# A decoder layer with routed experts: its opening in another order, with rows copied within SBUF, smaller pieces and ready-made constants

## What is computed

```python
x = x + attention(layernorm(x))        # 16 heads of 16, bias -|i - j| * 0.5 ** head, softmax over 1024 keys
x = x + cross_attention(layernorm(x))  # one head of 256, 77 context rows
x = x + experts(layernorm(x))          # 8 experts 256 -> 1024 -> 256, the two best per row
```

## Time and profile before

| | |
|---|---|
| median of 3 runs | 1537.01 us (1536.56 to 1537.97) |
| the profiled execution | 1541.59 us, its span 1539.7 us |
| mean granted TensorE clock | 0.981 of full speed |
| PE busy | 1481.3 us, 96% of the span |
| DVE, ACT, POOL busy | 1172.5, 1014.2, 415.0 us |
| first maximum's matmul / first score's matmul | 35.06 / 91.90 us from the span's start |

### The profile page before, as it was taken

One profiled execution on the slowest core, in us unless ns is written; L12 is line 12 of the kernel. 1 busy time (PEld: TensorE's weight loads), 2 busy tenths in 40 slices (PEclk: granted clock), 3 DMA queues, 4 the chain that ended last, 5 costly groups with the idle time before them and its releaser, 6 DMA issues.

```text
span 1539.7 us, 28797 instructions
## 1 busy us (share of the span) xinstructions
PE 1481.3 (96%) x9670; PEld 890.0 (58%) x9670; DVE 1172.5 (76%) x2578; ACT 1014.2 (66%) x1826; POOL 415.0 (27%) x457
## 2 busy tenths in 40 slices
PE   5899999999999999999999999999999999999997
PEld 3433443244444334444443444335999999999996
DVE  5889887788887778888877877854778887665563
ACT  3056666677655757665567575778677788776673
POOL 3200130002110014211003210023537655544453
PEclk9799999999999989999989999999999999999998
DMA  5750350330432504205042230133568888899993
GB/s 143 129 120 13 45 121 34 41 43 4 66 71 55 97 22 77 35 9 124 29 69 55 44 43 10 48 121 127 165 190 230 259 234 240 240 269 260 255 269 79
DMA packets 90404, 172.55 MB, mean 112 GB/s; under 512 B 14467, under 2 KB 48515, under 8 KB 90256
## 3 DMA queue, kind: packets, MB, share of 16 engines
q1 hardware_dynamic: 73120, 142.98, 37.0%
q0 software_dynamic: 15744, 26.54, 8.4%
q10 hardware_dynamic: 1392, 1.18, 0.4%
HBM read 134.27 MB, written 36.00 MB: 111 GB/s over the span
## 4 chain that ended last, share of the span: by engine, by line
PE 84%; DVE 8%; issue 3%; ACT 3%; DMA 1%; SPq 1%; POOL 0%; ACTq 0%; POOLq 0%; DVEq 0%
PE ps L1257 15%; PE ps L1231 15%; PE ps L1217 12%; PE ps L1459 4%; PE ps L1478 4%; PE ps L1479 3%; PE ps L1457 3%; PE ps L1458 3%; PE ps L1480 3%; DVE sums L1683 2%; PE ps L1363 2%; PE ps L1329 2%; PE ps L1220 2%; PE ps L1461 2%; PE ps L1276 1%
## 5 line engine op out<-in xcount | busy, mean ns | idle before, releaser
L1503 ACT ACTIVATE prob<-ps 128x512 f32<-128x512 f32 x1024 | 562.4, 606 | 305.2 <-PE ps L1217 175.0
L1257 PE MATMUL ps<-stacked_k,stacked_q 112*128 112x512 bf16 x1024 | 396.4, 393 | 17.1 <-DVE rmax L1683 4.0
L1683 DVE CUSTOM_DVE_ANT_0 sums<-ps,ramps 128x512 bf16<-128x512 f32 x480 | 328.9, 685 | 81.3 <-PE ps L1257 73.8
L1685 DVE TENSOR_REDUCE rmax<-ps 128x1 f32<-128x512 f32 x480 | 327.3, 687 | 73.7 <-PE ps L1257 69.3
L1217 PE MATMUL ps<-stacked_q,stacked_k 115*128 115x512 bf16 x1024 | 363.4, 384 | 4.2 <-ACT prob L1503 1.8
L1257 PEld LDWEIGHTS ps<-stacked_k,stacked_q 112*128 112x128 bf16 x1024 | 100.2, 99 | 334.8 <-DVE rmax L1683 117.7
L1231 PE MATMUL ps<-prob,values 128*32 128x512 f32 x2048 | 275.5, 610 | 1.3 <-issue 0.8
L2128 POOL DMA_INDIRECT out<-yo,token_of x71 | 139.6, 1966 | 189.8 <-DVE yo L2010 138.8
L1634 ACT ACTIVATE hid<-ps,w_now 128x256 f32<-128x256 f32 (+1 forms) x312 | 124.7, 452 | 88.3 <-PE ps L1459 59.6
L1217 PEld LDWEIGHTS ps<-stacked_q,stacked_k 115*128 115x128 bf16 x1024 | 99.8, 98 | 100.4 <-ACT prob L1503 53.9
L1478 PE MATMUL ps<-w_high,hid_high 128*128 128x256 f32 x512 | 149.1, 291 | 1.5 <-DVE sums L2004 1.5
(11 more groups left out here) (246 smaller groups left out, 2399.4 us busy)
## 6 DMA issues: line engine op xcount, KB each, us to landing
w_now<-in_w SPq DMA_DIRECT2D x78, 514.0 KB
w_now<-in_w SPq DMA_DIRECT2D x78, 512.0 KB
stacked_q<-parts_of_rows SPq DMA_DIRECT2D x90, 128.0 KB, 6.3
stacked_k<-parts_of_rows SPq DMA_DIRECT2D x90, 128.0 KB, 6.8
xi<-expert_rows SPq DMA_DIRECT2D x71, 130.0 KB, 3.0
parts_of_rows<-q_part SPq DMA_DIRECT2D x21, 256.0 KB, 5.6
parts_of_rows<-k_part SPq DMA_DIRECT2D x21, 256.0 KB, 5.7
b_now<-in_b SPq DMA_DIRECT2D x39, 128.0 KB
```

The costliest lines, as they stand in the source:

```text
L1257: m = e.matmul(ps[:, bank, :], qa[i][0:MAX_ROW, hh, qt * P:(qt + 1) * P], ka[i][0:MAX_ROW, hh, kc * BANK:(kc + 1) * BANK], start=True, sto ...
L1503: e.activation(prob[:, u % NPROB, :], ps[:, score_bank(u), :], ACT.Exp, scale=SLOPE ** (k[0] % NG * HG + k[3])).then_inc(sem["exp"], 1)
L1683: e.tensor_tensor_reduce(sums_16[:, :], of, ramp_beside(1 - qt % 2, qt % 4), 1.0, -3.0e38, ALU.add, ALU.max, into).then_inc(sem["maxed"], 1)
L1685: e.tensor_reduce(into, of, AX.X, ALU.max).then_inc(sem["maxed"], 1)
```

## The change

- **Layer norm in fours.** The statistics, reciprocal root and shift of sequence 0 are taken for tiles 0 to 3 and then for tiles 4 to 7; of the first four tiles ACT normalises two and DVE two (`normed`), and PE waits for each tile by itself.
- **Transfers of the opening.** The weights come in three pieces (q and k of heads 0 to 7, q and k of heads 8 to 15, values), the first between the rows' second and third transfer. The identity, the scales and the bias come from ACT's queue. The position rows are passed ready made in bf16 and go from the input to the stacks.
- **Rows without DRAM.** `direct` copies the parts of group 0 from SBUF to the stacks, 12 transfers for each half; five of them (q high and mid, first half) are started by POOL, the others by SP. Group 1's stacks are also filled from SBUF, in 12 transfers, and without a wait for the context's. To make that possible the channels of q and k are in the order (d, h) within a group; the later `spread` transfers therefore read 8 KB in one piece where it was four times 2 KB.
- **PE kept running.** 14 matmuls of 512 columns on zeros at the start and 5 after the first statistics. They write to a bank that nobody reads yet.
- **Order.** POOL no longer makes low parts of the weights; DVE does. The two projections of the other half (heads 0 to 7) stand behind the first rows. The eight context transfers go from POOL's queue to SP's, behind the 16 of the stacks 1 and 2 and group 1. The context products start after 32 maxima where it was 48.

```diff
+DIRECT = 2.8
+WARM, WARM_AFTER = 14, 5
...
-FIRST_ALONE = 3 * UNITS // 4
+FIRST_ALONE = UNITS // 2
+FIRST_BY_ACT = 2
...
+def by_pool(a, n, ch):
+    return a == 0 and n < 2 and ch == 0
...
     def prepare_first():
-        yield from layer_norm("pre", 0, WHOLE, FORE)
-        add("scale_q")
+        for tt in range(*FORE):
+            add("stats", "pre", 0, tt)
+        add("aggr", "pre", 0, FORE)
+        add("rstd", "pre", 0, FORE)
+        add("scale_q", 0)
         add("scale_bias")
         add("w_high", 0)
         add("w_low", 0)
+        add("shift", "pre", 0, FORE)
+        for tt in range(*FORE):
+            add("norm" if tt < FIRST_BY_ACT else "normed", "pre", 0, tt)
         for c in range(DC):
-            yield from x_parts(0, c, 0)
+            add("x_turn", 0, c, 0)
+            add("x_high", 0, c, 0)
+        for tt in range(*AFT):
+            add("stats", "pre", 0, tt)
+        for c in range(DC):
+            add("x_low", 0, c, 0)
+        add("aggr", "pre", 0, AFT)
+        add("rstd", "pre", 0, AFT)
+        add("specials")
+        for a in range(2):
+            for i in range(p.parts(("proj",))):
+                p.add_part(i, "proj", 0, 0, a, 0)
+            for n, kind in enumerate(("high", "rest", "mid", "low")):
+                add(kind, 0, 0, a, 0)
+                if kind != "rest":
+                    add("direct", a, n - (n > 0), 0)
+            if a == 0:
+                add("shift", "pre", 0, AFT)
         for tt in range(*AFT):
             add("norm", "pre", 0, tt)
-
-        yield from project(0, 0, 0, 0)
+        add("fill")
+        yield 0
         for c in range(DC):
-            yield from x_parts(0, c, 1)
-        yield from project(0, 0, 1, 0)
+            add("x_turn", 0, c, 1)
+            add("x_high", 0, c, 1)
+            empty("x_low", 0, c, 1)
+            yield 0
+        flush()
+        add("scale_q", 1)
         for i in range(1, DC + 1):
             add("w_high", i)
-            add("w_low_late", i)
+            add("w_low", i)
         for a in range(2):
             yield from project(0, 0, a, 1)
-        for ch in range(NCH):
-            add("first_half", ch)
+            flush()
+            for n in range(NPART):
+                add("direct", a, n, 1)
         split.add((0, 0))
-        now["spread"] = 1
         spread_when_ready()
+        add("context_in")
...
+        spec_rows = t["c_spec"].bitcast(BF16)
...
-        by_row = lambda rows: rows.rearrange("(h d) n -> d h n", d=DH)
+        by_row = lambda rows: rows.rearrange("(d h) n -> d h n", d=DH)
...
+        def direct_rows(e, a, n, ch):
+
+            cols, part = slice(ch * BANK, (ch + 1) * BANK), ("high", "mid", "low")[n]
+            if (a, n) == (1, 0) and ch == 0:
+                e.wait_ge(sem["k_ones"], 1)
+            rows = "early_rows" if by_pool(a, n, ch) else ("first_rows", "spread0")[ch]
+            e.wait_ge(sem[part], p.upto(part, 0, 0, a, ch))
+            for j, pair in enumerate(PAIRS):
+                if pair[a] == n:
+                    e.dma_start((qa, ka)[a][0][DH * j:DH * (j + 1), :, cols], split[n][a][first_group, 0, cols]).then_inc(sem[rows], 16)
...
+            rows_of_x(0)
+            rows_of_x(1)
+            piece_in(0)
+            rows_of_x(2)
+            rows_of_x(3)
+            e.dma_start(ramp_in, t["c_ramps"].rearrange("a p n -> p a n")).then_inc(sem["ramps_in"], 16)
+            position_rows(0)
+            for i in range(1, DC + 1):
+                piece_in(i)
+            e.dma_start(bv_all[:, :], t["bv"].broadcast_to([P, D])).then_inc(sem["values_bias_in"], 16)
...
+                elif kind == "context_in":
+
+                    e.wait_ge(sem["w_low"], DC + 1)
+                    for i, (w, b) in enumerate((("xwk", "xbk"), ("xwv", "xbv"), ("xwq", "xbq"))):
+                        e.dma_start(cw[i], t[w].rearrange("(c p) n -> p c n", p=P)).then_inc(sem["context_in"], 16)
+                        e.dma_start(cbias[i], t[b]).then_inc(sem["context_in"], 16)
+                    e.dma_start(cx[0:CTX, :, :], t["ctx"].rearrange("b c d -> c b d")).then_inc(sem["context_in"], 16)
+                    e.dma_start(xwo[:, :, :], t["xwo"].rearrange("(c p) n -> p c n", p=P)).then_inc(sem["context_in"], 16)
...
-                        e.wait_ge(sem["positions"], 32)
-                        e.wait_ge(sem["spread0"], spread_in(0))
-                        e.wait_ge(sem["context_in"], 8 * 16)
                         for other in range(1, NSET):
                             position_rows(other)
+                        for part in ("high", "mid", "low"):
+                            e.wait_ge(sem[part], p.upto(part, 0, 0, 1, NCH - 1))
+                        for j, pair in enumerate(PAIRS):
+                            for a, rows in enumerate((qa, ka)):
+                                e.dma_start(rows[1][DH * j:DH * (j + 1), :, :], split[pair[a]][a][next_group, 0, :]).then_inc(sem["spread1"], 16)
+                        continue
...
+            def warm(n):
+
+                for _ in range(n):
+                    e.matmul(ps[:, AV_BANK, :], sums_16[:, 0:P], sums_16[:, :], start=True, stop=True)
+
+            e.wait_ge(sem["first_set"], 1)
+            warm(WARM)
+            e.wait_ge(sem["aggr"], 1)
+            warm(WARM_AFTER)
...
-                    if (mo, a) == (0, 0) and first:
-                        e.wait_ge(sem["x_low"], p.upto("x_low", b, DC - 1, ch))
+                    if (mo, a) == (0, 0):
+                        e.wait_ge(sem["x_low"], p.upto("x_low", b, part, ch))
                     if b == 0 and first:
-                        if mo == 0:
-                            e.wait_ge(sem["w_low"], 1)
-                        else:
-                            e.wait_ge(sem["w_low_late"], 1)
+                        e.wait_ge(sem["w_low"], mo + 1)
...
+            e.dma_start(ident[:, :], t["c_ident"]).then_inc(sem["ident_in"], 16)
+            e.dma_start(scale_in, t["c_scale"].broadcast_to([P, D])).then_inc(sem["scale_in"], 16)
+            e.dma_start(scale_of, t["c_scale_of"]).then_inc(sem["scale_in"], 16)
+            e.dma_start(bqk[:, :, :], t["bqk"]).then_inc(sem["bias_in"], 16)
...
-            def first_keys(ch):
-                cols = slice(ch * BANK, (ch + 1) * BANK)
-                e.wait_ge(sem["first_k"], 16 * NPART * (ch + 1))
-                for j, (_, of_k) in enumerate(PAIRS):
-                    e.dma_start(ka[0][DH * j:DH * (j + 1), :, cols], by_row(stage[0, 1, of_k, 0:HG * DH, cols])).then_inc(sem[("first_rows", "spread0")[ch]], 16)
...
+                elif kind == "normed":
+                    which, b, tt = k
+                    i = lane(which)
+                    if tt == FIRST_BY_ACT:
+                        e.wait_ge(sem["shift"], p.upto("shift", which, b, FORE))
+                    e.tensor_scalar(xr_next[:, tt, :], xr_next[:, tt, :], rstd2[i][:, tt:tt + 1], shift2[i][:, tt:tt + 1],
+                                    ALU.mult, ALU.add).then_inc(sem["normed"], 1)
...
-            for i in range(NSET):
-                m = e.memset(ka[i][SPECIAL:P, :, :].bitcast(F32), TWO_ONES)
-            m.then_inc(sem["k_ones"], 1)
-            e.wait_ge(sem["k_ones"], 1)
+            def key_ones(i):
+                e.memset(ka[i][SPECIAL:P, :, :].bitcast(F32), TWO_ONES).then_inc(sem["k_ones"], 1)
+                e.wait_ge(sem["k_ones"], i + 1)
+
+            key_ones(0)
+            key_ones(1)
...
+                    e.wait_ge(sem["ramps_done"], 1)
+                    e.wait_ge(sem["rstd"], p.upto("rstd", "pre", 0, AFT))
+                    key_ones(2)
...
-        "c_spec": np.concatenate([kspec, qspec]),
+        "c_spec": (np.concatenate([kspec, qspec]).view(np.uint32) >> 16).astype(np.uint16).view(np.float32),
...
+    by_group = lambda v: v.reshape(-1, NG, HG, DH).transpose(0, 1, 3, 2).reshape(-1, DC, P)
+    q, k = (by_group(qkv[:, n]) for n in range(2))
+    qkv = np.concatenate([q[:, 0], k[:, 0], q[:, 1], k[:, 1], qkv[:, 2]], axis=1)
```

More of the change, by code:

```diff
@@ L672, in step_on @@
             parts.pop(0)
-    now = {"unit": 0, "ended": 0, "spread": 0, "maxima": 0, "running": False, "late": False}
+    now = {"unit": 0, "ended": 0, "spread": 1, "maxima": 0, "running": False, "late": False}
     placing, closing, staging, emptying, scattering = [], [], [], [], []
@@ L692, in bank_free @@
         before = p.holder.get(p.max_bank(place // UNITS, place))
-        return before is None or p.emptied["maxed", *before[1:]] <= p.pe + 0.1
+        return before is None or p.emptied.get((EMPTIED[before[0]], *before[1:]), float("inf")) <= p.pe + 0.1
     opening = prepare_first()
-    while ("x_low", 0, DC - 1, 0) not in p.number:
-        next(opening)
-    add("fill")
-    add("specials")
-    while not split:
-        next(opening)
+    next(opening)
     now["late"] = True
@@ L708, in plan, with rows_in @@
     landed = float("inf")
[L710 removed]
+    def rows_in():
```

(7 more changed lines are left out.)

151 lines of the change are left out of this document (60 added, 91 removed).

## The result

The changed kernel takes **1544.22 us** (median, 1543.13 to 1545.64), the kernel before 1536.78 beside it. The ratio is 1.0046, 95% interval 1.0037 to 1.0056: about 7 us **slower**, where I forecast 9.9 faster. The profiled execution took 1544.05 us with a span of 1542.2.

A forecast was written before the change was run, and what follows sets the result against it. PE, 96% busy, bounds the kernel from the first score on, so the opening's gain should arrive at the end: -10.9 + 1.0 = -9.9 us, 1537.01 to 1527.1 us by the median, range 1522.6 to 1532.5.

The forecast's parts named there:

- First maximum: Opening: first maximum at 21.5 us, 13.5 us earlier, the last transfer ahead of it POOL's.
- parts that cost nothing: Warm matmuls (at most 0.6 us), zeroing, ACT issues, wider descriptors, context loads landed near 48 with 3 us cover.
- Mid and low of k: Opening: k's two split steps take 0.43 and 0.69 us where POOL's weight splitting had made them 1.38 and 1.67.
- rival (b): Opening: each of POOL's issues waits for a DVE operation; 0.5 to 2 us arrive, 1527.6 to 1529; 12%.
- First to last reduction: Group 0's maxima on DVE: 51.9 us with 1 us taken back, last reduction at 74.9, 8.9 us earlier.
- three signs that I had named as fatal: DVE idling over 8 us in 32 reductions; PE waiting at next statistics; first score 11 us earlier but not the end.
- To the first score: Behind the last reduction: turn saves 2.4 us, net 2.0; first score at 81.0, 10.9 us earlier.
- For which I add 0.4: Maxima rows' transfers before the first score: 0.4 us added for 2 MB of x fetched beside them.
- 1.0 net: Behind the first score: two maxima fewer made ahead must be made up on DVE, 2 x 0.69, 1.0 us net.
- (d): Next sequence's fetch, now later on POOL, holds up its statistics on DVE; worst case 4 us late; slower; 3%.
- (a): Group 0's maxima: PE stays the later engine, mostly at the lower clock; gain 4.5 us, 1532.5; 12%.
- (e): Opening: copies into 16 partitions land like the slowest position rows, 7.2 us later; gain 4.2 us, 1532.8; 3%.

The follow-up runs named there:

- Both: The change with context transfers started ahead of group 1's copies and POOL's x fetches waiting for the maxima rows; ratio to the kernel before 0.9992.
- ACT's loads late: On "Both": ACT's three loads behind the identity wait until the second x transfer has landed; ratio to the kernel before 1.0011.
- Context first: The change with SP's eight context transfers started ahead of the 16 for groups 1 and 2; ratio to the kernel before 1.0015.
- fetch after rows: The change with POOL's two fetches of x waiting until the maxima rows have landed; ratio to the kernel before 1.0032.
- norms first: On "Both" with position rows behind the weights: ACT's loads held until the first x transfer, weights' steps behind the norms; ratio to the kernel before 0.9979.

## Why the prediction was wrong

The prediction ended at -9.9, the profile stands at +9.1 where the opening is over (the medians at +7.4). The 19.0 us between them, step by step: 5.3 at the first reduction (28.25 for 23), 7.6 from there to the last (59.5 us for 51.9), 4.2 from `nmax` to the first score (10.3 for 6.1), 1.9 behind it. "Both" takes back 12.2 of them. The other 6.8 are 5.4 at the first reduction, 0.4 from there to the last, -0.2 to the first score and 1.2 behind it.

**First maximum.** "Without waiting for the last two transfers the first four tiles' statistics end at about 5.0" failed: they ended at 8.2. I had costed four transfers; what ACT's queue now issues beside them stood under "parts that cost nothing". The held loads brought them back to 5.3. From norm to projection I had 3.3 us, it was 3.46. "At twice the clock 1.5" failed: q's six matmuls took 3.0 (14.26 to 17.29) at the lower clock, after pauses of 2.5, 0.4 and 0.6 us. q's low part was ready at 20.0 for 15.4. What followed was sized well: 8.25 us from there to DVE's first reduction, 7.6 predicted. The rows themselves were not late: they landed 2.4 to 3.2 us after issue (2.9 predicted), and the first maximum stood behind six projection matmuls of tiles 4 to 7 (24.13 to 26.86), not behind POOL's row as I had it.

**Mid and low of k** at 0.43 and 0.69: they took 0.47 and 0.69. POOL's issues took 0.51 each beside them:

```profile
L1084 POOL DMA_DIRECT2D stacked_q<-q_part x5: 512/514/765, 18.3 to 20.6; - x5
```

So rival (b) did not come about; a POOL issue beside DVE's casts and two-input operations was shorter than the 0.74 beside its reductions.

**First to last reduction.** This is the term that turned the sign. 51.9 us was right for the work: in "both", where the context is in time, it was 28.39 to 80.7, 52.3. The step that failed is under "parts that cost nothing": "24 x 0.46 = 11 us, landed near 48 ... three us are their cover". I had timed the queue by its issues. The last load landed 14.9 us later than forecast (62.9 for 48). SP came to the 24 transfers 5.7 us later than I had it (37.7 for 32), the issues took 16.6 us for 11 (0.60 for each copy), and from their end to the landing it was 8.6 us for 5. PE wanted the loads 5.9 us later too (56.9 for 51), so a cover of 3 became a wait of 6.0. What weighs most is that what was issued ahead had not landed: sixteen transfers into 16 partitions each, 2.1 MB, need 16 to 20 us at 105 to 130 GB/s, and the context stood behind them in the same queue. At that rate quicker issues alone would have gained little.

Before, `xwo` was issued at nearly the same time, 51.4 for 52.4 now, and its loads landed 2.6 to 4.7 us after their issue. But nothing slow was on its way beside them: SP started the 16 transfers only when the context had landed, and the change took that wait out. SP's wait in the profile of before, 20 to 100 us (in its code it waits for the context there):

```profile
SPq L1098 <- DMA xwo<-in_xwo: 18.2, 1, 18.2
```

The only queue with packets from 46 to 56 us was POOL's (packets, MB, share):

```profile
q0 software_dynamic: 606, 1.62, 59.1%
```

"Context first" shows that the order within SP's queue is enough for the 5.85 us. Whether the loads would have been quick on POOL's queue with SP's copies beside them, no run here tried.

The Trainium skill has the rule that I did not look for: "SBUF — State Buffer", section "Door 1: The DMA port swizzle", gives the rate by the partitions that a transfer reaches, 104 GB/s measured into partitions 0 to 15 against 328 into all 128. The trace agrees: 105 GB/s is the commonest slice while the copies ran, and 231 to 319 when the context's full-width loads came. By that rule 2.1 MB take 20 us, an estimate, from 38 to 58; in the trace the fast slices begin at 56.8. The context's 1.4 MB behind them, at 231 to 319 GB/s, end near 63, where 62.9 was measured.

The clock added little: with `xwo` in time the first four products still took 2.42 us, as at the lower level of the earlier trace rows. Of the three signs that I had named as fatal, the first came: DVE idled 14.2 us among its reductions. In "both" it still idled 7.1 where it was 6.3 before, so the 1 us that I took back for a better spread of the products is not there either.

**To the first score.** The turn did as predicted: `nmax` to `nrow_of` 0.60 us instead of 3.1, a saving of 2.5 (2.4 predicted). "For which I add 0.4" failed by a factor of ten: the fetches made it 4.6 (5.7 us against 10.3 from `nmax` to score). I had seen 2 MB as a share of the bandwidth; the 8 KB rows landed 7.0 us after their issue, 1.9 in the median of all groups. The fetches had been issued 2.2 and 1.3 us before the first of them, on POOL's queue, when POOL had seen the last context product; with the fetches held back ("fetch after rows") the wait was gone. Before, the next sequence's fetch went at 52.2 and the residual's at 89.8, behind the rows' first issue (88.34).

**Behind it.** "1.0 net" for two maxima fewer: from the first score to `nmax` of group 1 it is 48.3 us, before 45.4, so 2.9. In "both", which waits for almost nothing there, it is 47.6. Put together, `nmax` of group 0 to that of group 1 takes 53.5 us in "both" and 53.5 before: the shorter way to the first score gave nothing at all. DVE, which has the second group's maxima to reduce, is busy 47.1 and 46.7 of these 53.5 us; that it sets the pace there is my reading, no run tested it. I had counted 2.0 - 1.0 for it.

**Rivals.** The slower one, (d), named the fetch, but as a late one for the next statistics; they were not waited for. The true ones were a fetch too early and a load behind slow copies. (a) supposed the lower clock through the maxima; from 35 to 60 us it was 0.99. (e) had the slow landing, but for group 0's rows; it was group 1's, twelve of them behind four position rows, that took 6.0 to 11.0 us.

## What to carry to other kernels

When transfers change their place in the queues, or a wait between them goes, time them by landing: from the bytes ahead of them and the partitions that these go to, not by the issues. When a wait disappears, ask which fetch is released by it at the very moment at which a few KB are on the critical path; one wait cost 1.1 us elsewhere and gave back 4.8 at `nmax` of group 1. And check a shortened latency at a mark behind the next bound engine, not at the place where it is saved.

## What was new about the hardware

- A load that copies one DRAM row of 1 KB to 128 partitions (128 KB), issued at 1.2 us on ACT's queue, delayed the second 256 KB transfer of SP's queue: the statistics that need it began at 7.3 to 8.1 us. Issued at 3.7 to 4.5 it did not, and they began at 4.5 or earlier. From 3.5 to 4.0 us all DMA engines together moved 61 to 129 GB/s with it and 287 to 340 without.
- Loads of 1 and 2 KB, 8 and 16 bytes for each of 128 partitions (the expectations call them 4-byte pieces), took 8.3 and 8.2 us from issue to landing when they were issued at 4.9 and 5.4 beside the weights ("ACT's loads late").
- Copies from SBUF into 16 partitions took SP 0.60 us each to issue (0.46 from DRAM) and landed in 2.4 to 3.2 us for group 0 (64 KB each), in 6.0 to 11.0 for group 1 (128 KB each, a row of twelve behind four position rows).
- PE's clock was 1.00 (2.4 GHz) up to 12 us with the warm matmuls running up to the transposes, and still fell to the lower level after five matmuls of the projection, behind a pause of 2.3 us in which PE waited for the weights' low part. Behind a pause of 3.9 us ("norms first") the projection ran at the lower level from its start.
